# The last two batches of an attention and feed-forward kernel, handled tile by tile

## The reference

```python
x = x + xattn(layernorm(x), ctx_768, Wq, Wk, Wv, Wo, bo)
# second part
h = layernorm(layernorm(x), g1, b1n)
h = bitlinear(h, w1, b1)                 # 256 -> 1024 columns
h = gelu(h)
h = layernorm(h, g2, b2n)                # over 1024 columns
h = bitlinear(h, w2, b2)                 # 1024 -> 256 columns
x = x + h

def act_quant_fake(x):                   # inside bitlinear, one scale for each row
    scale = 127.0 / clip(max(abs(x), axis=-1), 1e-5)
    return clip(round(x * scale), -128, 127) / scale
```

## Time and profile before

| | |
|---|---|
| median of three executions | 1171.8 us (1171.19 to 1174.75) |
| the profiled execution | 1175.15 us, of which the span is 1173.4 us |
| DVE's last instruction ends (L733) | 1157.72 us from the span's start |
| last product ends (L1138) | about 1166.5 us |
| last DMA is issued (L525) | 1167.64 us |
| mean granted TensorE clock | 0.981 of full |

### The profile page before, as it was taken

One profiled execution on the slowest core, in us unless ns is written; L12 is line 12 of the kernel. 1 busy time (PEld: TensorE's weight loads), 2 busy tenths in 40 slices (PEclk: granted clock), 3 DMA queues, 4 the chain that ended last, 5 costly groups with the idle time before them and its releaser, 6 DMA issues.

```text
span 1173.4 us, 34309 instructions
## 1 busy us (share of the span) xinstructions
PE 1021.2 (87%) x12162; PEld 731.5 (62%) x12208; DVE 1022.4 (87%) x1579; ACT 834.9 (71%) x2152; POOL 690.4 (59%) x927
## 2 busy tenths in 40 slices
PE   5999999999999999999999866877777777777775
PEld 4777777777777777777777533544444444444443
DVE  1588989988888888888888899999999999999994
ACT  3555555665566666666664657999999999999992
POOL 3345555754455555555556456766666666666666
PEclk8999999999999999999999988999999999999997
DMA  4558767666778875665775401333333233333335
GB/s 138 137 132 167 144 152 147 146 146 143 149 135 154 157 148 145 146 141 142 144 146 117 107 19 22 40 38 37 36 36 36 36 36 36 36 36 36 36 36 64
DMA packets 144451, 114.30 MB, mean 97 GB/s; under 512 B 51548, under 2 KB 134876, under 8 KB 144376
## 3 DMA queue, kind: packets, MB, share of 16 engines
q1 hardware_dynamic: 126248, 95.85, 37.8%
q0 software_dynamic: 17408, 16.78, 12.3%
q10 hardware_dynamic: 720, 0.66, 0.2%
HBM read 71.23 MB, written 33.63 MB: 89 GB/s over the span
## 4 chain that ended last, share of the span: by engine, by line
PE 36%; DVE 21%; issue 20%; DMA 10%; SPq 7%; POOL 3%; ACT 1%; DVEq 1%; POOLq 0%; ACTq 0%
DMA r_rows<-x_r 9%; DVE gn_low L754 7%; DVE gn_high L754 7%; PE banks L1229 6%; PE banks L1216 6%; PE banks L1148 4%; PE banks L1193 4%; SPq L365 4%; PE banks L1159 3%; PE banks L1168 3%; PE banks L1179 2%; DVE gn_low L740 2%; PE banks L1181 2%; POOL gn_low L515 1%; DVE g_max L760 1%
## 5 line engine op out<-in xcount | busy, mean ns | idle before, releaser
L900 ACT ACTIVATE probs<-banks 120x512 f32<-120x512 f32 x256 | 132.1, 602 | 84.4 <-PE banks L1198 84.4
L646 DVE TENSOR_REDUCE nm_part<-banks 128x16 f16<-128x1920 f32 x64 | 138.1, 2158 | 35.3 <-PE banks L1148 35.1
L497 POOL TENSOR_TENSOR f_r<-f_ve,neg_half 128x2 f32<-128x2 f32 x62 | 43.7, 706 | 206.2 <-DVE f_ve L691 204.7
L943 ACT ACTIVATE g_dev<-g,g_sum 128x1024 bf16<-128x1024 f32 x128 | 149.7, 1169 | 0.0
L948 ACT ACTIVATE g<-banks,h_dq 128x1024 f32<-128x1024 f32 x128 | 142.7, 1135 | 7.7 <-PE banks L1100 7.7
L1136 PE MATMUL banks<-w_t,g_t 128*128 128x256 bf16 x1024 | 125.2, 276 | 14.5 <-ACT g_t L975 11.0
L1229 PE MATMUL banks<-wo_sb,o_t 128*128 128x256 f32 x512 | 128.2, 394 | 5.9 <-DVE o_t L788 5.9
L1136 PEld LDWEIGHTS banks<-w_t,g_t 128*128 128x128 f16 x1024 | 96.7, 99 | 54.5 <-issue 30.5
L1216 PE MATMUL banks<-xt,wq_c 128*128 128x256 f32 x512 | 126.8, 391 | 0.0
L1094 PE MATMUL banks<-w_t,h_t 128*128 128x512 bf16 x466 | 116.4, 385 | 5.3 <-issue 1.7
L1229 PEld LDWEIGHTS banks<-wo_sb,o_t 128*128 128x128 f32 x512 | 94.4, 195 | 24.6 <-DVE o_t L788 6.3
(11 more groups left out here) (149 smaller groups left out, 2711.9 us busy)
## 6 DMA issues: line engine op xcount, KB each, us to landing
x_in<-in_x SPq DMA_DIRECT2D x64, 256.0 KB, 4.1
xt<-in_x_t SPq DMA_DIRECT2D x64, 256.0 KB, 3.6
xr<-in_x SPq DMA_DIRECT2D x64, 256.0 KB, 5.8
out<-xr SPq DMA_DIRECT2D x64, 256.0 KB, 6.5
out<-res POOLq DMA_DIRECT2D x64, 256.0 KB, 4.4
r_bc<-r_rows SPq DMA_DIRECT2D x64, 128.0 KB, 4.9
ctx_t<-in_ctx_t SPq DMA_DIRECT2D x64, 120.0 KB, 3.0
w_raw<-in_w_t SPq DMA_DIRECT2D x8, 256.0 KB, 5.3
```

The costliest lines, as they stand in the source:

```text
L646: dve.tensor_reduce(nm_part[:, q, :, 0:T * C], s_p, AX.X, ALU.max, negate=True).then_inc(max_done, 1)
L900: act.activation(probs[:, p, j, :, :], sc_p[:, j, :, :], ACT.Exp, scale=SCALE).then_inc(probs_done, 1)
L943: act.activation(g_dev[:, t, :], g[:, p, t, :], ACT.Square, scale=-float(F), bias=g_sum[:, p, t:t + 1], accum_out=g_ssq[:, p, t:t + 1]).th ...
```

## The change

Everything up to batch 61's products stays as it is. What follows is written out:

- DVE: the last reduction is split by tile, each followed by a reciprocal and a product with 127 (a new one-column constant `top`), so that the scale of batch 63 is made on DVE. DVE then quantises tile 1 of batch 63 itself, and makes the results of batches 62 and 63 in one instruction for each tile: product times `g_dq` plus the rows of `xr`.
- POOL quantises the other three tiles; its accumulating stores end with batch 61.
- PE takes tile by tile, in another order; batch 63 has banks of its own, bank 3 and the first of `pair_a`.
- ACT copies batch 63's transposed rows to a buffer of their own (`g_t_last`, in the place of an unused one).
- SP stores the results of batches 62 and 63 by tile, as plain transfers over what the first part had left in the output.

```diff
@@ sync
+                def store_last(b, t, count):
+                    sp.wait_ge(last_out, count)
+                    sp.dma_start(out[b].rearrange("(t p) n -> p t n", p=P)[:, t, :], res[:, b % 4, t, :]).then_inc(last_stored, 16)
+                for n, b in enumerate((NB - 2, NB - 1)):
+                    for t in range(T):
+                        store_last(b, t, n * T + t + 1)
+                sp.wait_ge(last_stored, 16 * 2 * T)
@@ gpsimd (out_scale, quantise_rows, store: the same instructions as before, as functions)
-                steps(pool, 4, FFN_END + 1, FFN_L0, FFN_L1, ffn, 4)
+                steps(pool, 4, NB - 1, FFN_L0, FFN_L1, ffn, 4)
+                pool.wait_ge(g_affine, NB * T)
+                pool.wait_ge(gqs_done, NB - 1)
+                out_scale(NB - 2, 2)
+                for t in range(T):
+                    quantise_rows(t, 2)
+                pool.wait_ge(last_qs, 1)
+                quantise_rows(0, 3)
+                store(NB - 5, 3)
+                pool.wait_ge(last_max, T)
+                out_scale(NB - 1, 3)
+                store(NB - 4, 0)
+                store(NB - 3, 1)
                 for r in range(4):
-                    pool.wait_ge(stored[r], NB * 4)
+                    pool.wait_ge(stored[r], NB * 4 if r < 2 else NB * 4 - 16)
@@ vector
+                dve.memset(top[:, :], QMAX).then_inc(s_const, 1)
...
-                steps(dve, 4, NB, FFN_L0, FFN_L1, ffn, 4)
+                steps(dve, 4, NB - 1, FFN_L0, FFN_L1, ffn, 4)
+                centre(NB - 1, 3)
+                dve.wait_ge(gr_done, NB)
...
+                for t in range(T):
+                    dve.wait_ge(g_affine, (NB - 1) * T + t + 1)
+                    dve.tensor_reduce(g_max[:, 3, t:t + 1], gn_floored[3][:, t, :], AX.X, ALU.max,
+                                      apply_absolute_value=True).then_inc(last_max, 1)
+                    dve.wait_ge(last_max, t + 1)
+                    dve.reciprocal(g_inv[:, 1, t:t + 1], g_max[:, 3, t:t + 1]).then_inc(last_inv, 1)
+                    dve.wait_ge(last_inv, t + 1)
+                    dve.tensor_tensor(g_qs[:, 1, t:t + 1], g_inv[:, 1, t:t + 1], top[:, :], ALU.mult).then_inc(last_qs, 1)
+                dve.wait_ge(last_qs, T)
+                dve.tensor_scalar(gn[3][:, 1, :], gn[3][:, 1, :], g_qs[:, 1, 1:2], MAGIC_H, ALU.mult, ALU.add).then_inc(last_quant, 1)
+                def add_residual(b, t, r, y):
+                    dve.scalar_tensor_tensor(out=res[:, r, t, :], in0=y[t], scalar=g_dq[:, r, t:t + 1],
+                                             in1=xr[:, r, t, :], op0=ALU.mult, op1=ALU.add).then_inc(last_out, 1)
...
+                dve.wait_ge(gdq_done, NB)
+                for t in range(T):
+                    add_residual(NB - 2, t, 2, y2_tiles)
+                dve.wait_ge(stored[3], (NB - 4) * 4)
+                for t in range(T):
+                    dve.wait_ge(last_y, t + 1)
+                    add_residual(NB - 1, t, 3, y2_last)
@@ scalar
-                steps(act, 4, FFN_END, FFN_L0, FFN_L1, ffn, 4)
+                steps(act, 4, NB, FFN_L0, FFN_L1, ffn, 4)
+                for t in range(T):
+                    residual(NB - 3, t, 1)
+                gelus_turned(NB - 2)
+                for t in range(T):
+                    act.wait_ge(gt_ps, (NB - 1) * T + t + 1)
+                    act.activation(g_t_last_words[:, t, :], gt_words[:, t, :], ACT.Copy).then_inc(gt_done, 1)
@@ tensor
-                steps(pe, 4, FFN_END, FFN_L0, FFN_L1, ffn, 4)
+                steps(pe, 4, NB, FFN_L0, FFN_L1, ffn, 4)
+                pe.wait_ge(gq_done, (NB - 2) * T + 1)
+                turn_gelus(NB - 2, 0, 2)
+                pe.wait_ge(out_done, (NB - 2) * T)
+                rows_down(NB - 2, 0, y2_tiles, g_t, True)
+                pe.wait_ge(gq_done, (NB - 2) * T + 2)
+                turn_gelus(NB - 2, 1, 2)
+                pe.wait_ge(gq_done, (NB - 1) * T + 1)
+                turn_gelus(NB - 1, 0, 3)
+                rows_down(NB - 2, 1, y2_tiles, g_t, False)
...
+                rows_down(NB - 1, 0, y2_last, g_t_last, True)
...
+                pe.wait_ge(last_quant, 1)
+                turn_gelus(NB - 1, 1, 3)
+                rows_down(NB - 1, 1, y2_last, g_t_last, True)
```

More of the change, by code:

```diff
@@ L98, in xattn_ffn @@
         w_out = sb("w_out", [P, 1])
+        top = sb("top", [P, 1])
         bias_mov = sb("bias_mov", [P, F], BF16)
@@ L500, in attn, with store, out_scale, quantise_rows @@
                         quantise(b, (n + 1) % 4)
+                def store(b, r):
+                    pool.wait_ge(out_done, b * T + T)
+                    pool.dma_start(out[b].rearrange("(t p) n -> p t n", p=P), res[:, r, :, :],
+                                   accum_op=ALU.add).then_inc(stored[r], 16)
+                def out_scale(b, r):
+                    pool.tensor_tensor(g_dq[:, r, :], g_max[:, r, :], w_out[:, 0:1].to_broadcast([P, T]),
+                                       ALU.mult).then_inc(gdq_done, 1)
+                def quantise_rows(t, r):
+                    p = r % 2
+                    pool.tensor_scalar(gn[r][:, t, :], gn[r][:, t, :], g_qs[:, p, t:t + 1], MAGIC_H,
+                                       ALU.mult, ALU.add).then_inc(gq_done, 1)
                 def ffn(j, n):
@@ L523, in ffn @@
                     if live(b, NB):
[L524 to L526 removed]
+                        store(b, r)
                 def power(b, m):
@@ L1107, in turn_bias, with turn_gelus, rows_down @@
                               start=True, stop=True).then_inc(bt_ps, 2)
+                def turn_gelus(b, t, r):
+                    after(pe, gt_done, (b - 1) * T + t + 1)
+                    for f in range(FC):
+                        last = pe.transpose(gt_p[:, t, f, :], gn_half[r][:, t, 2 * f * P:2 * (f + 1) * P:2], ident_h[:, :])
+                    last.then_inc(gt_ps, 1)
+                def rows_down(b, t, y, turned_rows, first):
+                    pe.wait_ge(gt_done, b * T + t + 1)
+                    for f in range(FC):
+                        pe.matmul(y[t], turned_rows[:, t, f, :], w2_t[:, f, :],
+                                  start=(first and f == 0), stop=False, skip_group_check=True)
                 def ffn(j, n):
@@ L1119, in ffn @@
                             pe.wait_ge(gq_done, b * T + t + 1)
-                            after(pe, gt_done, (b - 1) * T + t + 1)
-                            for f in range(FC):
-                                last = pe.transpose(gt_p[:, t, f, :],
-                                                    gn_half[r2][:, t, 2 * f * P:2 * (f + 1) * P:2], ident_h[:, :])
-                            last.then_inc(gt_ps, 1)
+                            turn_gelus(b, t, r2)
                     b = j + 2
@@ L1133, in ffn @@
                         for t in range(T):
-                            pe.wait_ge(gt_done, b * T + t + 1)
-                            for f in range(FC):
-                                pe.matmul(y2_p[:, t, :], g_t[:, t, f, :], w2_t[:, f, :],
-                                          start=(t == 0 and f == 0), stop=False, skip_group_check=True)
+                            rows_down(b, t, y2_tiles, g_t, t == 0)
                         pe.matmul(y2_p, neg_one[:, :], w2_sum[:, :].unsqueeze(1).to_broadcast([P, T, D]),
```

34 lines of the change are left out of this document (28 added, 6 removed).

## The result

| | before | changed |
|---|---|---|
| median of 7 runs each | 1171.19 us (1169.53 to 1174.75) | 1164.94 us (1162.49 to 1168.68) |
| ratio | | 0.9948, 95% interval 0.9926 to 0.9970 |
| profiled execution | 1175.15 us | 1168.3 us |
| its span, mean granted clock | 1173.4 us, 0.981 | 1166.6 us, 0.982 |

The kernel became 6.1 us faster (the interval reaches from 3.5 to 8.7 us).

A forecast was written before the change was run, and what follows sets the result against it. The prediction took the emptying chain after batch 61's products as what counts; terms 0.4 + 0.4 + 0.2 + 2.5 = 3.5 us off the median 1171.8 gave 1168.3 us, range 1166.2 to 1171.6.

The forecast's parts named there:

- almost none of that busy time is at stake: Whole kernel: DVE and PE are 87% busy, but the change touches only what follows batch 61's products.
- the layout rival: All 64 batches: `top` moves the tiles behind it, changing instruction or transfer times; 10%, 6% slower and 4% faster.
- the loops hold the same instructions: Both parts' loops: with shapes and types also unchanged, no row speaks for a slowdown from moved tiles.
- One more memset at the start: Start of the kernel: the added memset, with four issues on SP's queue, costs nothing on the chain.
- Term 1: PE's last products: batch 62's tile 0 starts 1.5 us earlier, but the last product ends only 0.4 us earlier.
- Terms 2 and 3: Last product to last issue: one DVE result instead of an ACT pair, 0.4 us; SP issuing instead of POOL, 0.2 us.
- Term 4: Last transfer: a plain 128 KB store lands in 2.0 us instead of 4.5 us, a gain of 2.5 us.
- so little is queued: Last store's issue, at 1166.6: earlier stores have mostly drained, so 2.0 us was taken for the landing.
- the stores land late: Rival on the last transfers, 15%: accumulating and plain stores crowd; gain 1.0 us (1170.8), or a time of 1172.8 us.
- the tail behind the landing, 1.3 us, stays: From last landing to end of span: 1.3 us before and after the change, no gain.
- The forecast's clock: PE in the tail: granted clock kept as profiled, half (1.2 GHz) from 1158.7 to 1162.1, then full.
- The sign that I had written down for a changed body: DVE's last large reduction starting later than 1155.2 would mean the kernel's body changed and the sum says nothing.

The follow-up runs named there:

- e3: The kernel before with one more memset at the start of VectorE's program, no tile moved; loop 419.52 us, ratio 0.9990.
- e5: The changed kernel with the memset of `top` given by GpSimd instead of VectorE; loop 421.53 us, tail 20.75 us, ratio 0.9972.
- e2: The kernel before with the tile `top` declared but never used, so tiles behind it move; loop 421.50 us, ratio 0.9995.
- e4: The changed kernel with `top` declared behind all other tiles, which lie where they lay before; loop 419.51 us, ratio 0.9951.
- f2: The changed kernel with GpSimd, too, waiting for the four last plain stores; tail 21.28 us, ratio 0.9950.
- f1: The changed kernel with GpSimd's store of batch 59 issued ahead of batch 62's scale and quantising; tail 20.57 us, ratio 0.9946.
- e1: The kernel before, unchanged, run a second time; loop 421.52 us, tail 25.00 us, ratio 1.0006.
- e6: The kernel before with only VectorE's results of batches 62 and 63 and SyncE's plain stores of them; tail 21.80 us, ratio 0.9974.
- e7: The changed kernel with batch 63's reduction whole, scale on ScalarE and both quantisings on GpSimd, as before; tail 21.84 us, ratio 0.9956.
- f3: The changed kernel with a second memset at the start of VectorE's program; loop 419.53 us, ratio 0.9950.
- f4: The kernel before with VectorE's results, SyncE's plain stores and one memset at VectorE's start; loop 419.53 us, tail 21.70 us, ratio 0.9952.
- e8: The changed kernel with eight unread products added on PE around the transposes of batch 62's tile 0; tail 21.46 us, ratio 0.9945.

## Why the prediction was wrong

**The step that failed** is "almost none of that busy time is at stake", and with it, in the layout rival, that "the loops hold the same instructions". They do, and the loop still lost 2.0 us (421.51 to 419.53). The cause is the memset of `top`: in the part costed at nothing stands "One more memset at the start", and by e3 and e5 this instruction alone takes the loop from one time to the other, on either kernel. I looked for its cost on the chain at the start, and not for what it does to the loop behind it. With these 2.0 us the sum would have been 5.5 us, 1166.3 us, and the measured 1164.94 would stand 1.4 us below it; the medians of the kernel before, 1171.8 then and 1171.19 now, explain 0.6 of these, and the other 0.8 us lie within the interval of the measured gain (3.5 to 8.7 us).

Do the times agree with the marks? Alone the memset gave 0.1% (1.2 us, interval 0 to 2.3), the tail alone 0.28% (3.3 us), both together 0.49% (5.7 us, e4). The difference of 1.2 us lies within the intervals; the marks say 2.0 + 3.4, less about 0.2 given back in batches 0 to 4.

**The layout rival** had 10% (4% faster) and named a cost in each of 64 batches. The side of it that came true is the faster one, but its mechanism, addresses of tiles, fell with e2 and e4, and the size is 0.034 us a batch.

**The tail** came out at 3.4 us, beside the forecast's 3.5, by luck: its errors cancelled. Term 1 was mis-sized by 0.2: the products started when the walk said, and the clock fell and rose about 0.8 us earlier than it had. Terms 2 and 3 measured 0.6 us for 0.6. Term 4 was mis-sized most, 1.4 instead of 2.5: I had "so little is queued", while the changed kernel's windows show a DMA share of 1.10 and 0.88 around the last issue, at 1163.1. The row behind the 2.0 was also read too kindly: the 1.4 us of full engines in the earlier trace rows moved 0.38 MB at 269 GB/s, so more than the one store of 0.26 MB went through them. The case "the stores land late" was the right thing to fear, at part of its price. And "the tail behind the landing, 1.3 us, stays" was wrong by 0.8 us; f2 shows that it belongs to the engine that waits, and the change moved that wait.

**Clock.** The forecast's clock was right for this execution (low in the first stretch, high after), but that too is chance. Before, after, e5 and f1 fell to half at 10.0 to 10.8 us behind m62, under the products; e1, e3, e6 and e7 stayed at 1.00; e2, e4, f2, f3 and f4 fell at 4.6 to 6.1 us and were back before the products. The last product ended at 18.5 (before) and 17.9 in the first group and at 16.7 to 17.2 us in the other two. What follows behind, though, takes most of it back: last issue and landing run against each other (e1 18.40 and 5.4, before 19.71 and 4.5; e4 18.08 and 3.7, e8 18.59 and 2.5), so the tail differs by less than the clock's 1.3 us.

**What held:** products of 62 tile 0 at 1157.89 by before's times (said 1157.9); reductions of 1.22 and 1.21 us (1.2), VectorE's quantising of 0.75 us (0.75), the result 0.48 us (0.45); and that the scale and quantising by tile are worth nothing that can be measured (e7). The quantising fell into GpSimd's issue of the store of batch 59, as forecast (1155.38 and 1155.29), and that issue took 1.17 us as in the earlier trace rows, so no delay shows. The sign that I had written down for a changed body, a last large reduction of DVE later than 1155.2, could not show a body that is shorter.

## What to carry to other kernels

An edit that adds or removes an instruction ahead of a hardware loop can change that loop's time although no instruction in it changes: measure a kernel with the instruction alone before giving its gain to the edit, and try one instruction more ahead of a long loop. In a tail, cost the last transfer by what is still queued at its issue, and let the last wait be SyncE's. An engine that ends earlier buys little while the transfers behind it have not drained.

## What the runs showed of the hardware

- One or two VectorE instructions more ahead of its loop take 0.13 us off each of twelve passes, 0.11 of it at one instruction, and 0.37 off the first; the loop takes 421.50 to 421.53 us in five profiles without such an instruction (before, e1, e2, e5, e6) and 419.51 to 419.54 in nine with one or two. What in the chip does it stays open: that the idle time stands at one fixed instruction of each pass speaks for the reading of the instructions, but no run tells that apart from other causes.
- From the last landing to the end of the span pass 1.2 us where GpSimd alone waits for it, 0.4 where SyncE alone does and 1.0 where both do (f2).
- The same bytes cost the DMA engines 2.6 times more as GpSimd's accumulating stores than as SyncE's plain ones (33% and 12.5% of 25 us for a MB). Whether that is the adding or the queue was not tried apart.
- A product of one column on VectorE took 0.19 us in the tail and 0.67 us where GpSimd was quantising beside it (1154.67, L921 above). The Trainium skill ("SBUF — State Buffer", two separate sides) says that the two engines take a shared pair of ports by an exclusive lock, for a whole instruction. The trace agrees: the long one ends at 1155.34, 0.01 us behind GpSimd's instruction. The other product, at 1153.12, also stood beside GpSimd's work and took 0.19, but it started where one GpSimd instruction gave way to the next, within 0.02 us. At that same place it took 0.19 us in e4, e5 and f2 too, and 1.13 us in e8, f1 and f3, again to the end of GpSimd's next instruction.
